# Low products of the attention scores: 64 rows of q and k in place of 128 rows of which half are zeros

## What is computed

```python
q = (hidden_states @ Wq).reshape(b, s, HEADS, HEAD_DIM)
k = (hidden_states @ Wk).reshape(b, s, HEADS, HEAD_DIM)
...
logits = jnp.einsum('bhqd,bhkd->bhqk', q, k)
causal = jnp.tril(jnp.ones((s, s), dtype=bool))[None, None]
logits = jnp.where(causal, logits, MASK_VAL)
logits = logits / jnp.sqrt(jnp.float32(HEAD_DIM))
attn = jax.nn.softmax(logits, axis=-1)
out = jnp.einsum('bhqk,bhkd->bhqd', attn, v)
```

## Time and profile before

| | us |
|---|---|
| median of 3 runs (1061.97 to 1062.54) | 1062.06 |
| the profiled execution | 1062.15 |
| its span | 1060.3 |
| TensorE matmuls busy (PE) | 1042.1 |
| TensorE weight loads busy (PEld) | 865.9 |
| VectorE busy (DVE) | 758.5 |
| ScalarE busy (ACT) | 639.0 |
| GpSimd busy (POOL) | 416.1 |

### The profile page before, as it was taken

How to read it: one execution, slowest core, us unless ns; L and a number is a source line. 1 busy time by engine, 2 the same in 40 slices (tenths; PEclk the granted TensorE clock), 3 DMA queues, 4 the chain that set the end, 5 groups by cost and what they waited for, 6 DMA issues and landing times.

```text
span 1060.3 us, 20102 instructions
## 1 busy us (share of the span) xinstructions
PE 1042.1 (98%) x5495; PEld 865.9 (82%) x5495; DVE 758.5 (72%) x2138; ACT 639.0 (60%) x1454; POOL 416.1 (39%) x422
## 2 busy tenths in 40 slices
PE   7999999999999999999999999999999999999996
PEld 6888888888888888888888888888887888888884
DVE  8677777776666767666666767666667777777777
ACT  6667777776665766666665656666685333334333
POOL 4153443434252544434352534434466232233221
PEclk9999999999999999999999999999999999999999
DMA  7122324232311346021011202021232323332311
GB/s 279 40 85 71 129 69 134 69 130 59 101 56 30 109 169 228 16 71 50 30 49 35 69 10 69 10 74 48 92 132 59 120 80 100 119 111 87 99 60 61
DMA packets 58663, 90.36 MB, mean 85 GB/s; under 512 B 3568, under 2 KB 36336, under 8 KB 58608
## 3 DMA queue, kind: packets, MB, share of 16 engines
q1 hardware_dynamic: 58464, 89.44, 25.7%
q10 hardware_dynamic: 144, 0.26, 0.1%
HBM read 64.52 MB, written 25.17 MB: 85 GB/s over the span
## 4 chain that ended last, share of the span: by engine, by line
PE 94%; DVE 1%; ACT 1%; issue 1%; POOL 1%; DVEq 0%; ACTq 0%; POOLq 0%
PE bank L1477 50%; PE bank L1408 24%; PE bank L1508 6%; PE bank L1527 3%; PE bank L1526 3%; PE bank L1642 2%; PE bank L1619 1%; PE bank L1450 1%; PE bank L1643 1%; PE bank L1529 1%; PE bank L1493 1%; PE bank L1438 1%; POOL big_lo L660 1%; PE bank L1420 0%; DVE stats L1187 0%
## 5 line engine op out<-in xcount | busy, mean ns | idle before, releaser
L1477 PE MATMUL bank<-big_hi,w_hi 128*128 128x512 f32 (+1 forms) x776 | 325.8, 420 | 0.3 <-DVE big_lo L1037 0.3
L597 POOL TENSOR_SCALAR prob<-prob,rinv 128x128 f32<-128x128 f32 (+3 forms) x256 | 136.6, 533 | 445.7 <-DVE rinv L1072 445.0
L1477 PE MATMUL bank<-big_hi,w_lo 128*128 128x512 f32 (+1 forms) x776 | 304.5, 392 | 0.0
L1477 PE MATMUL bank<-big_lo,w_hi 128*128 128x512 f32 (+1 forms) x776 | 302.8, 390 | 0.0
L742 ACT ACTIVATE prob<-prob,nmax 128x128 f32<-128x128 f32 (+3 forms) x256 | 143.9, 562 | 212.1 <-DVE nmax L1062 210.3
L1477 PEld LDWEIGHTS bank<-big_hi,w_lo 128*128 128x128 f32 x776 | 145.6, 188 | 32.8
L1477 PEld LDWEIGHTS bank<-big_hi,w_hi 128*128 128x128 f32 x776 | 146.5, 189 | 19.7 <-issue 0.4
L1477 PEld LDWEIGHTS bank<-big_lo,w_hi 128*128 128x128 f32 x776 | 147.1, 190 | 11.6
L1062 DVE CUSTOM_DVE_ANT_0 prob<-bank,mask 128x256 f32<-128x256 f32 (+2 forms) x192 | 106.1, 553 | 35.4 <-PE bank L1408 28.0
L1080 DVE TENSOR_TENSOR pT_lo<-bank,pT_hi 128x128 fp32r<-128x128 f32 (+3 forms) x256 | 124.3, 486 | 2.6 <-ACT pT_hi L753 2.4
L1508 PE MATMUL bank<-ident,prob 128*128 128x128 f32 x640 | 111.7, 272 | 1.3 <-DVE pT_lo L1080 0.8
(11 more groups left out here) (148 smaller groups left out, 1894.5 us busy)
## 6 DMA issues: line engine op xcount, KB each, us to landing
w_raw<-in_wqkv SPq DMA_DIRECT2D x48, 512.0 KB, 4.5
attention_out<-o_sum SPq DMA_DIRECT2D x64, 128.0 KB, 2.3
w_raw<-attention_out SPq DMA_DIRECT2D x16, 512.0 KB, 4.7
land<-in_x SPq DMA_DIRECT2D x16, 512.0 KB, 3.5
out<-res SPq DMA_DIRECT2D x14, 512.0 KB, 2.6
xin<-in_x SPq DMA_DIRECT2D x12, 512.0 KB, 5.7
xT_hold_hi<-xin SPq DMA_DIRECT2D x8, 512.0 KB, 3.6
xT_hold_lo<-xn SPq DMA_DIRECT2D x8, 512.0 KB, 5.4
```

The lines of the kernel that those rows point to most:

```text
L597: pool.tensor_scalar(p, p, rinv[:, q % 4:q % 4 + 1], 1.0, ALU.mult, ALU.mult).then_inc(prob_done, 1)
L1477: done = pe.matmul(grp_ps[(b + k) % 2][:, cols], w, xt[:, cols], start=at == 0, stop=at == GROUP_MM - 1)
```

## The change

The low product of query tiles 1 to 3 reads 64 rows of `q_hl` and `k_lo`, the head's own, in place of all 128. The high product and the combined product of tile 0 are as before, and so are the zeros that tile 0 still reads. The two matmuls are written out in place of the call of the helper; the semaphore is raised by the second, as before.

```diff
                     else:
-                        products(sc_ps[q % 2][:, kc], [(q_hl[:, ab, h, qc], k_hh[:, ab, h, kc]),
-                                                       (q_hl[:, ab, h, qc], k_lo[:, ab, h, kc])], True, True
-                                 ).then_inc(s_done, 1)
+                        own = slice(DH * h, DH * h + DH)
+                        pe.matmul(sc_ps[q % 2][:, kc], q_hl[:, ab, h, qc], k_hh[:, ab, h, kc], start=True, stop=False)
+                        pe.matmul(sc_ps[q % 2][:, kc], q_hl[own, ab, h, qc], k_lo[own, ab, h, kc], start=False, stop=True
+                                  ).then_inc(s_done, 1)
```

## The result

| | before | after |
|---|---|---|
| median, us | 1062.05 | 1134.78 (1134.41 to 1135.22) |
| profiled execution, its span | 1062.15, 1060.3 | 1134.54, 1132.7 |

The changed kernel takes 72.7 us more: ratio 1.0684, 95% interval 1.0668 to 1.07. For each of the 384 changes between 128 and 64 rows that is 72.7 / 384 = 0.189 us on average, for each low product 0.379 us.

A forecast was written before the change was run, and what follows sets the result against it. TensorE's matmul stream, busy for 98% of the span, was taken to bound the kernel. With 0 for columns, loads and row changes, the profiled 1062.15 us stayed, forecast as 1062.0 us, range 1059 to 1123.

The forecast's parts named there:

- Going from 128 rows to 64 and back: Around each low product, 384 changes of row count: taken as costing nothing, with bounds of 12, 61 and 134 us.
- Loads are covered: Weight loads of low products run under the matmul streaming meanwhile, so a cheaper load gains nothing; taken as 0.
- the third rival: Loads of 64 rows, or full ones behind them, aren't made ahead: up to 0.35 us a change, 1123 to 1196; chance 0.10.
- The second rival: TensorE empties its array at each of 384 row changes: 12 to 61 us more, up to 1123 us; chance 0.34.
- The columns streamed: Low score products hold TensorE by their columns, 33 us in all; 64 rows stream no faster, gain taken as nothing.
- The last rival: Fewer rows let columns of low products pass at the granted clock: 2.4 us less, 1059.6 us; chance 0.08.
- Everything else: Matmul, load and semaphore counts, waits, zeros and transfers elsewhere in the kernel stay as before: cost nothing.
- Nothing hides what TensorE loses: In the score stretch, 45 to 805 us, TensorE has no slack: a nanosecond added there is one at the end.

The follow-up runs named there:

- The two halves: Against the changed kernel, the low product of the 512-column tile cut into two 64-row matmuls of 256 columns, one behind the other; 1134.33 us.
- the pair of narrow products: Against the changed kernel, the high product also uses only the head's own 64 rows, like the low one; 1137.5 us.

## Why the prediction was wrong

**The step that failed** is "Going from 128 rows to 64 and back", where it says of the row nearest in kind, the 64-column product: "its price is nothing. I take nothing." A change of rows costs 0.189 us, and 384 of them the 72.7 us. L1526 and L1527 change the number of stationary columns; that row was no test of a change of rows, and the prediction had said itself that it "says little if these don't count as a change of mode". Columns don't bring the price: those products kept their pace after the change, and 64 rows by 64 columns cost less than 64 by 128, by the smaller load.

**"Loads are covered"** failed with it, at the loads on either side of a change: 192 of 64 rows and the 192 behind them. All others, but for 13 behind other waits, still start ahead of their own matmul. It was the third rival, with a chance of 0.10, that had the place and both parts of the mechanism; its 1123 to 1196 us hold the time, and the range ended at its lower border. Its upper price, 0.35 us a change, was too large in both terms: emptying 0.08 to 0.09 and not 0.16, since the next load doesn't wait for the modelled end of the matmul (it starts at 542.97, the high product's end is 542.65 + 0.39 = 543.04); and load 0.107 and not 0.19, since in the rows a matmul starts with its load and not behind it (542.97 for both). The rate of loads in the earlier trace rows, 0.12 us, was the better row for it, and was read there for another purpose. With the 0.09 us that only the trace after shows, it would have given 384 x 0.21 = 81 us.

**The second rival**, emptying alone, had half the mechanism: it would be 384 x 0.08 = 31 us, 1093. The Trainium skill (TensorEngine Tiling (Array Packing), Key Properties) says that a change of tiling mode drains TensorE. The runs agree: 64 and 32 rows pay, 96 doesn't, and narrow matmuls among themselves don't. The products of 64 stationary columns pay nothing, and whether they count as a mode no run shows. Nor does any show whether a change between 64 and 32 rows would pay.

**The columns streamed** were right: the narrow product streams at the old pace. The two halves of 0.43 us show it, which are 0.23 of columns and one price, and so does the pair of narrow products, whose second one takes 0.23 us at 512 columns in the chain:

```profile
505.99 0.23 PE bank L1498
```

The last rival, a faster column, has no support.

**Everything else** was right but for some 3 us: TensorE is busy in all of the stretch, the part behind the attention kept its 255 us, and the other engines' busy time stayed. The bound from the profile, that a nanosecond on TensorE's stream is one at the end, held for 72.7 of the 76 us that the chain shows. "Nothing hides what TensorE loses" overlooked a little slack, the waits of weight loads for the turned probabilities in the stretch (L1508 from 45 to 805 us before, L1509 from 45 to 877 after):

```profile
PEld bank L1508 <- issue: 2.0, 6, 0.5
PEld bank L1508 <- POOL prob L597: 1.7, 3, 0.8
...
PEld bank L1509 <- issue: 0.9, 4, 0.3
```

They shrank by 2.8 us, which is about what is missing; no run tests that it is this.

## What to carry to other kernels

Using 64 of 128 rows saves no time on TensorE by itself, and each change between 128 and 64 (or 32) rows in a stream of matmuls costs some 0.19 us here: rows of zeros were the cheaper way. If narrow matmuls are wanted, put them one behind the other, so that several share two changes (two did here); or use more than 64 rows (96, the one number tried, went at nearly the full rate). And where a trace has no row for an operation, look for what it shares with the nearest row, here the columns and not the rows, before its price is taken over.

## What the runs showed of the hardware that wasn't expected

A change between 128 rows and 64 costs in two parts, 0.08 to 0.09 us of emptying and a load that isn't made ahead, an estimated 0.107 us for 128 stationary columns and 0.054 less for 64. A weight load's row is 0.19 us long, but an uncovered load holds the matmuls up by some 0.11 only (543.40 to 543.74, less 0.23 of columns). And a slower TensorE showed as a slightly busier one: its first matmul behind each change has a longer modelled row (502 ns for the low product of 512 columns, 391 before in the earlier trace rows), so its share of the span didn't fall but went from 98.3% (1042.1 of 1060.3 us) to 98.5% (1116.1 of 1132.7). The share of the weight loads fell from 82% to 76%.
